# Flamingo-style gated block, one core: ScalarE copies v ahead of the norm's seed; the last slots are reordered

## What is computed

```
for i in range(DEPTH):                       # DEPTH = 6
    x = attn_layer(shift_tokens(x), Wqkv[i], q_scale[i], k_scale[i], Wo[i]) + x
    x = ffn_layer(shift_tokens(x), ln_g[i], ln_b[i], W1[i], b1[i], W2[i], b2[i]) + x

def attn_layer(x, Wqkv, qs, ksc, Wo):        # 16 heads of 64, window 32
    q, k, v = split(x @ Wqkv)
    q = l2norm(q) * qs;  k = l2norm(k) * ksc
    q, k = rotary(q), rotary(k)              # cos and sin products, then their sum
    return local_attention(q, k, v) @ Wo     # softmax over 64 keys of each 32-token window

def ffn_layer(x, ...):
    xn = layer_norm(x);  a, gate = split(xn @ W1 + b1)
    return a * gelu(gate) @ W2 + b2
```

## Time and profile before

| | |
|---|---|
| median of 3 runs | 1777.94 us (1777.28 to 1783.73) |
| the profiled execution: its time | 1781.41 us |
| its span, first to last instruction | 1779.4 us |
| PE busy | 1709.0 us, 96% |
| ACT busy | 1396.2 us, 78% |
| DVE busy | 1370.6 us, 77% |
| POOL busy | 1499.9 us, 84% |
| table loads on ACT | 50 in all, 24 each at L714 and L718 |
| mean granted clock of PE | 0.986 of full speed |

### The profile page before, as it was taken

How to read it: one execution, slowest core, us unless ns; L and a number is a source line. 1 busy time by engine, 2 the same in 40 slices (tenths; PEclk the granted TensorE clock), 3 DMA queues, 4 the chain that set the end, 5 groups by cost and what they waited for, 6 DMA issues and landing times.

```text
span 1779.4 us, 48666 instructions
## 1 busy us (share of the span) xinstructions
PE 1709.0 (96%) x18122; PEld 1136.8 (64%) x18122; DVE 1370.6 (77%) x2399; ACT 1396.2 (78%) x2746; POOL 1499.9 (84%) x1204
## 2 busy tenths in 40 slices
PE   8689999999999999999999999999999999999996
PEld 7356666666666666666666666666666666666663
DVE  5687877778778777877887778787777877877773
ACT  3577878878779788788788787887887887877862
POOL 4799898888888988988988889889889888888860
PEclk8899999999999999999999999999999999999998
DMA  4022222222322223222223222222222222222221
GB/s 117 21 75 74 74 63 70 62 74 72 84 60 71 68 57 82 74 69 73 66 61 85 66 74 74 59 61 78 77 73 64 72 61 60 60 71 58 58 65 30
DMA packets 155273, 120.59 MB, mean 68 GB/s; under 512 B 42607, under 2 KB 151457, under 8 KB 154913
## 3 DMA queue, kind: packets, MB, share of 16 engines
q1 hardware_dynamic: 155041, 117.48, 24.9%
HBM read 18.79 MB, written 1.05 MB: 11 GB/s over the span
## 4 chain that ended last, share of the span: by engine, by line
PE 75%; ACT 13%; POOL 5%; issue 4%; DVE 3%; ACTq 0%; DVEq 0%; POOLq 0%
PE qk_bank L374 13%; PE ring_bank L470 9%; PE sc_bank L421 8%; PE ring_bank L446 8%; PE ring_bank L387 7%; PE ring_bank L514 5%; PE ring_bank L459 5%; PE ring_bank L434 5%; PE ring_bank L408 4%; PE ring_bank L525 4%; PE ring_bank L397 3%; ACT sq L616 2%; ACT L718 2%; POOL turned L1047 2%; POOL turned L1054 2%
## 5 line engine op out<-in xcount | busy, mean ns | idle before, releaser
L1047 POOL TENSOR_TENSOR turned<-qkn,tables 128x512 f32<-128x512 f32 x384 | 490.4, 1277 | 162.1 <-DVE qkn L844 159.3
L1054 POOL TENSOR_TENSOR turned<-qkn,tables 128x512 f32<-128x512 f32 x384 | 498.2, 1297 | 0.0
L374 PE MATMUL qk_bank<-wqkv,xT 128*128 128x512 f32 x768 | 363.5, 596 | 4.4 <-DVE qkn L852 4.4
L827 DVE TENSOR_REDUCE ss<-sq 128x16 f32<-128x1024 f32 x192 | 234.0, 1219 | 116.9 <-ACT sq L616 116.6
L1083 POOL TENSOR_TENSOR turned<-turned 128x512 f32<-128x512 f32 x192 | 254.6, 1326 | 15.1
L892 DVE TENSOR_TENSOR o<-ring_bank,rr 128x512 f32<-128x512 f32 x192 | 132.6, 691 | 169.1 <-PE ring_bank L446 167.6
L1090 POOL TENSOR_TENSOR turned<-turned 128x512 f32<-128x512 f32 x192 | 244.5, 1273 | 15.0
L692 ACT ACTIVATE oT<-ring_bank 128x512 f32<-128x512 f32 x192 | 114.5, 596 | 179.5 <-PE ring_bank L459 179.3
L446 PEld LDWEIGHTS ring_bank<-vw,pT 128*32 128x32 f32 x6144 | 156.7, 110 | 143.7 <-issue 143.6
L656 ACT ACTIVATE kB<-ring_bank 64x512 f32<-64x512 f32 x384 | 225.8, 588 | 23.4 <-PE ring_bank L408 21.2
L421 PE MATMUL sc_bank<-kB,qT 128*32 128x128 f32 x6144 | 204.1, 273 | 8.9 <-ACT qT L647 8.9
(11 more groups left out here) (170 smaller groups left out, 2975.2 us busy)
## 6 DMA issues: line engine op xcount, KB each, us to landing
vw<-vs SPq DMA_DIRECT2D x1152, 64.0 KB, 2.0
vw<-vs SPq DMA_DIRECT2D x672, 32.0 KB, 1.9
wqkv<-in_L_ffn_Wqkv_dram SPq DMA_DIRECT2D x20, 384.0 KB, 3.5
wo<-in_L_ffn_Wo_dram SPq DMA_DIRECT2D x20, 128.0 KB, 3.3
w<-in_L_ffn_W_dram SPq DMA_DIRECT2D x6, 341.0 KB, 3.3
wqkv<-in_L_ffn_Wqkv_dram SPq DMA_DIRECT2D x1, 1536.0 KB, 10.3
x<-in_x_dram SPq DMA_DIRECT2D x2, 512.0 KB, 4.4
out_dram<-x SPq DMA_DIRECT2D x4, 256.0 KB, 2.3
```

Of the source, the lines that this page charges most:

```text
L374: mm = pe.matmul(QK[u % 2][:, i * UW:(i + 1) * UW], tok, wqkv[:, layer % 2, cut:cut + UW], start=True, stop=True)
L827: dve.tensor_reduce(ss[:, u % 2, :], heads(sq[:, :]), AX.X, ALU.add).then_inc(ss_done, 1)
L1047: return pool.tensor_tensor(heads(turned[:, u % 2, 2 * i, :]), heads(qkn[:, u % 2, i * UW:(i + 1) * UW]), table.unsqueeze(1).to_broadcast( ...
L1054: return pool.tensor_tensor(halves(turned[:, u % 2, 2 * i + 1, :]), halves(qkn[:, u % 2, i * UW:(i + 1) * UW])[:, :, ::-1, :], table.rearr ...
```

## The change

Five edits, in the order of the diff:

- PE: `keep_warm`, new, issues products of the constant tile mean_w with itself into a bank of QK that is free by then, for the last group only: 18 ahead of its first `up`, 8 ahead of its `variance`.
- PE: `transpose_out(g - 3)` stands in slot s = 1, between the transposes of the output and of the probabilities, no longer in slot 0 ahead of the transpose of q.
- ACT: `norm_seed(n - 1)` stands behind `copy_v(n)` instead of ahead of it, and so also behind `square_d` (s = 1) and `gelu_table` (s = 3). In slot 191 alone `squares` follows the seed directly.
- DVE: `finish(g - 3)` goes from slot 1 to slot 2, ahead of `add_eps`.
- DVE: in slot s = 0 `add_ffn(g - 3)` stands ahead of `sum_squares(n - 1)`.

```diff
--- before.py
+++ after.py
@@ -496,6 +496,13 @@
                 pe.matmul(RING[i % RINGS][:, :], mean_w[:, :], xT[:, g % B, 0:N],
                           start=True, stop=True).then_inc(ring_made[i % RINGS], 1)
 
+            def keep_warm(g, n):
+                if g != GROUPS - 1:
+                    return
+                pe.wait_ge(qn_done, UNITS)
+                for _ in range(n):
+                    pe.matmul(QK[0][:, 0:P], mean_w[:, :], mean_w[:, :], start=True, stop=True)
+
             def variance(g):
                 if not 0 <= g < GROUPS:
                     return
@@ -543,16 +550,20 @@
                 attend(n - 5)
                 scores(n - 3)
                 transpose_o(n - 6)
+                if s == 1:
+                    transpose_out(g - 3)
                 transpose_p(n - 4)
                 if s == 0:
                     mean(g - 2)
                 if s == 2:
                     fold_bias(g - 2)
                 if s == 3:
+                    keep_warm(g - 2, 18)
                     up("gate", 1, g - 2, 0)
                     up("gate", 1, g - 2, 2)
                 transpose_k(n - 2)
                 if s == 1:
+                    keep_warm(g - 2, 8)
                     variance(g - 2)
                 if s == 2:
                     project_out(g - 1, 0)
@@ -567,8 +578,6 @@
                     project_out(g - 1, 1)
                 if s == 7:
                     down(g - 2)
-                if s == 0:
-                    transpose_out(g - 3)
                 transpose_q(n - 2)
 
 
@@ -729,19 +738,22 @@
             for n in range(SLOTS):
                 g, s = n // UPG, n % UPG
                 copy_qT(n - 3)
-                norm_seed(n - 1)
                 if s == 1:
                     square_d(g - 2)
                 if s == 3:
                     gelu_table(g - 2)
                 copy_v(n)
+                norm_seed(n - 1)
+                if n == UNITS - 1:
+                    squares(n)
                 copy_oT(n - 6)
                 copy_pT(n - 4)
                 if s == 3:
                     gelu(g - 2, 0)
                     gelu(g - 2, 2)
                 copy_kB(n - 2)
-                squares(n)
+                if n < UNITS - 1:
+                    squares(n)
                 if s == 2:
                     rstd_seed(g - 2)
                 if s == 3:
@@ -981,9 +993,9 @@
                 invert_sum(n - 5)
                 less_maxima(n - 4)
                 if s == 1:
-                    finish(g - 3)
                     centre(g - 2)
                 if s == 2:
+                    finish(g - 3)
                     add_eps(g - 2)
                 if s == 3:
                     add_bias(g - 2)
@@ -991,9 +1003,9 @@
                     gated(g - 2, 2)
                 if s == 6:
                     gated(g - 2, 1)
-                sum_squares(n - 1)
                 if s == 0:
                     add_ffn(g - 3)
+                sum_squares(n - 1)
                 if s == 3:
                     add_attention(g - 1, 0)
                     rstd_newton(g - 2)
```

## The result

The changed kernel takes 1860.22 us in the median of 4 runs (1853.39 to 1862.77), the kernel before 1778.47 us (4 runs). The ratio is 1.0441, with a 95% interval of 1.0422 to 1.0460: slower by 82 us, where 52 were forecast. The profiled execution is the fastest of the four, 1853.39 us with a span of 1851.3 us. Its first product for q and k starts 51.3 us after the first instruction, that of the profiled execution before after 56.9; over the profiles of all runs here this lies between 51.3 and 58.2 us, with no relation to the edits that I can see. So profiles are compared here by distances between units, not by their spans.

What follows compares the result with a forecast made beforehand. PE was taken as the bound, busy 71.18 of 72 us a group. The terms 63.8 - 11.3 + 2.2 + 0.5 + 0.9 - 1.0 - 0.5 - 2.3 sum to +52.3 us, so 1830 us against 1777.9, range 1803 to 1862.

Steps and rivals of the forecast that it cites:

- Rival 2: PE's waits close together let the clock fall in every group: 33 us over 22 groups, 1863 us; 10%.
- Rival 3: The late seed makes POOL's chain the next wait, 1 us a group instead of 0.1: 1850 us; 10%.
- Three loads in slot 3: Three more ACT table loads in 22 groups, 3.85 us less idle time absorbed, delay PE by 2.9 each: +63.8 us.
- The seed behind the copy of v: All slots: PE's wait for v's copy goes in slot 1, -11.3 us; the later seed costs 0.1 in 22 groups, +2.2.
- The start: While the kernel starts, POOL has no slack and the first seed waits for v: +0.5 us, a copy's length.
- add_ffn ahead of sum_squares: Slot 0: the sum comes up to 1.5 us later, hidden because the seed waits for v anyway: 0.
- The last slots: Groups 20 to 22 and last group: +0.9 (group 20's variance waits 2 to 3 us), -1.0, -0.5, -2.3; sum -2.9 us.
- the gates behind the constant products: Last group: 18 constant products in PE's idle stretch keep full clock for the six gate products behind: -2.3 us.
- the variance: Last group: centre no longer waits for finish, 1.6 us, but eight constant products stand ahead of the variance: -0.5 us.
- Rival 1: ACT's spare time covers the loads in slot 3 and only the gains stay: some 1764 us; 3%.
- Rival 4: Each extra table load costs as much again, a drain of 1.28 us more in 22 groups: 1915 us; 2%.
- Rival 5: Only two of the three extra loads in slot 3 act, one serving Ln and Exp: 1802 us; 5%.

Runs made afterwards that it cites:

- E5: The kernel before with the changed order in slot 3 alone (Gelu load, copy of v, seed; 116 loads), seed first in all other slots: 1843.53 us.
- E9: The changed kernel with its 116 loads, and the seed first again in slot 1 alone: 1843.66 us.
- E6: E1 with the seed first again in slot 1 alone: 1786.30 us.
- E8: The kernel before, seed first, v copied ahead of square_d in slot 1, transposed result behind q's transpose, centre ahead of finish, constant products kept: 1773.07 us.
- E10: The kernel before with the seed behind the copy of v in the first 16 slots only: 1781.69 us.
- E7: The changed kernel with ACT's order of before in all slots, leaving the last-slot edits and add_ffn ahead of sum_squares: 1777.18 us.
- E2: The kernel before with, in slot 3 alone, the order Gelu load, seed, copy of v; 116 loads: 1867.98 us.
- E3: The kernel before with three more table loads right ahead of the Gelu load in slot 3, the seed left in place; 116 loads: 1905.90 us.
- E1: The changed kernel with the Gelu load moved behind the seed in slot 3, so 50 loads as before: 1808.78 us.

## Why the prediction was right, and where it was not

- *Direction and range.* Slower was forecast with 94%, and 1860.2 us lies within 1803 to 1862, at its upper end. The forecast's own value was 30 us too low. The range reached so far because rivals 2 (1863 us) and 3 (1850) were to lie in it for the most part, and neither happened as written: that the measured time is inside by 2 us is in part luck. A group grew by 3.60 us, within the 1.5 to 4 that the forecast named.
- *Three loads in slot 3, +63.8.* Shown right by E5: 62.7. The idle time between the old loads absorbed as much as was read from it. The waits for the output's copy and for a Gelu came where they were named.
- *The seed behind the copy of v, -11.3 + 2.2.* This is the step that failed. Undone in slot 1, it gives 18.2 us (E9) to 23.8 us (E6). In the steady part alone, from unit 16 to unit 191, the changed kernel takes 14.8 us more than E5, which has the same loads and no late seed in the other slots: in place of a gain of 9 a loss of 15, which is 24 of the missing 30. The start, 4.1 us for 0.5, may be most of the rest. I looked for the closest place of the chain behind the seed and took POOL's slack for the unit of slot 3, 1.01 us. In slot 1 the seed goes behind two instructions, square_d and the copy of v, and comes 1 us later, not 0.6, and the next product for q and k needs the bank that DVE empties behind the seed. The trace of before shows 1.31 us of slack there; the late start then met a row of POOL, which made DVE's step 0.9 us longer, so the scaling came 1.9 us later in the slot in the group shown. I had counted the gain of that slot (0.54; in E8, where only square_d goes behind v, it is 0.34) and not asked what the same slot's seed delays.
- *Rival 3* (the late seed makes POOL's chain the next wait, 10%) was the nearest to what happened, with its price of 1 us a group; its place was two slots off.
- *The start, +0.5.* 1.5 measured with an interval from -0.2 to 3.2 (E10). Open.
- *add_ffn ahead of sum_squares, 0.* E7 shows slot 0 unchanged.
- *The last slots, -2.9.* -3.6 (E7). Of its parts the gates behind the constant products gave 2.35 for 2.3 forecast, the variance 0.6 for 0.5 (4.12 us behind the mean, 4.68 before). The variance of group 20 waited 3.27 us, where 2 to 3 were forecast, and 1.47 in E7, where the seed is not late.
- *Rival 2* (the clock falls in every group) did not happen in the change, and did in 11 groups of E2 and 20 of E3, with the same loads placed ahead of v. *Rivals 1, 4 and 5* fell: of the loads' 3.85 us only 0.87 was absorbed, a load costs about its 1.28 us, and all three act.

## What to carry to other kernels

- Where an activation's table set is switched by hand, look at the built order for loads that nobody wrote; one activation moved across a load can make three.
- A step moved behind another is late by all that stands between them in each slot, so its chain has to be read in the slot where most stands there, up to the bank that its result frees.
- The same 66 loads cost 62.7, 88.5 or 126.4 us, by where they stood in the queue. Ahead of the first copy that PE waits for they leave ACT's later idle time unused, and PE's wait comes in one piece, behind which the clock fell in half of the groups or more.

## What was not expected of the hardware

- One wait of 2.37 us on PE was followed by a granted clock of 0.50 in 11 of 22 groups of E2, with 3.3 us for a pair of gate products instead of 1.9, and by 1.00 in the other 11; one of 3.67 by 0.50 in 20 of 22 (E3). In slot 3 of the changed kernel (waits such as 0.75, 0.56 and 0.92 us) and of E5 (1.54 and 0.92) it stayed at 1.00 in all 22.
- A DVE instruction of 128x16 with operands in SBUF (the newton step) takes 0.17 us when POOL is idle and up to 1.25 us when POOL has just begun a row; it ends some 0.03 us after POOL's row. In the mean over 192 steps that was 402 ns before and 733 ns after, though neither the instruction nor POOL's work had changed, only their phase.
- Two costs in the same slot need not add. Without the extra loads the late seed of slot 1 lengthens slot 3 by 0.60 us (E1 against E6); with them by nothing (the changed kernel and E9 both have 12.80).
